# Attention on one core: the row totals are inverted in four pieces of 128 columns, two of them earlier in the macro step

## The reference

```python
h = _L0_tok_ref(x, L0_tok_weight)
scores = jnp.einsum('bqhe,bkhe->bhqk', q, k) / math.sqrt(D_HEAD)
scores = jnp.where(causal[None, None], scores, -jnp.inf)
pattern = jax.nn.softmax(scores, axis=-1)
z = jnp.einsum('bhqk,bkhe->bqhe', pattern, v)
h = h + attn_out                      # attn_out = z @ W_O + b_O, on _layernorm(h)
h = h + _L0_ffn_ref(_layernorm(h), ...)
```

## Time and profile before

| | |
|---|---|
| median of 3 runs | 2627.59 us (2624.28 to 2630.31) |
| profiled execution | 2633.09 us, of which the span of the instructions is 2631.4 us |
| PE busy over the span | 2369.2 us (90%), granted clock 0.963 on average |
| DVE busy | 1876.9 us (71%) |
| ACT and POOL busy | 1245.0 and 1245.7 us (47% each) |
| the inversions (L973) | 96 of 128 x 256, 167.5 us in all |

### The profile page before, as it was taken

One profiled execution on the slowest core, in us unless ns is written; L12 is line 12 of the kernel. 1 busy time (PEld: TensorE's weight loads), 2 busy tenths in 40 slices (PEclk: granted clock), 3 DMA queues, 4 the chain that ended last, 5 costly groups with the idle time before them and its releaser, 6 DMA issues. The chain is left out here.

```text
span 2631.4 us, 42687 instructions
## 1 busy us (share of the span) xinstructions
PE 2369.2 (90%) x16192; PEld 1254.9 (48%) x16192; DVE 1876.9 (71%) x3802; ACT 1245.0 (47%) x1760; POOL 1245.7 (47%) x858
## 2 busy tenths in 40 slices
PE   3564899999999999999999999986999999999998
PEld 1233556665656565656565665543333333333332
DVE  7864665756565756656565656687988888988987
ACT  3322233333333333333333333345777777787776
POOL 5000265767675757675766666653413413323120
PEclk9786999999999999999999999996999999999999
DMA  1002000000001000000000001132011001000000
GB/s 50 12 15 62 1 8 7 3 10 1 9 1 33 1 10 1 10 1 9 1 10 1 10 1 20 19 52 56 9 19 27 9 19 21 15 19 17 11 7 7
DMA packets 42941, 39.35 MB, mean 15 GB/s; under 512 B 26865, under 2 KB 35186, under 8 KB 41842
## 3 DMA queue, kind: packets, MB, share of 16 engines
q1 hardware_dynamic: 40608, 31.18, 5.4%
q0 software_dynamic: 1536, 3.15, 0.4%
q10 hardware_dynamic: 594, 2.31, 0.2%
HBM read 26.13 MB, written 10.49 MB: 14 GB/s over the span
## 5 line engine op out<-in xcount | busy, mean ns | idle before, releaser
L690 POOL TENSOR_TENSOR acc<-acc,pT 128x1024 f32<-128x1024 f32 (+3 forms) x412 | 837.9, 2034 | 228.5 <-ACT pT L1131 191.6
L1131 ACT ACTIVATE pT<-banks 128x1024 f32<-128x1024 f32 x480 | 406.8, 896 | 803.9 <-PE banks L769 758.3
L1868 DVE TENSOR_TENSOR hw<-hid,banks 128x512 f32<-128x512 f32 x1024 | 662.8, 680 | 86.4 <-PE banks L1551 71.9
L930 DVE TENSOR_REDUCE part<-banks 128x2 f32<-128x1024 f32 (+3 forms) x432 | 438.3, 1044 | 300.5 <-PE banks L745 298.6
L1710 ACT ACTIVATE hid<-banks 128x1024 f32<-128x1024 f32 x512 | 496.6, 1022 | 186.4 <-PE banks L1541 169.6
L785 PE MATMUL banks<-pT,v 128*64 128x512 f32 (+3 forms) x1920 | 405.7, 543 | 0.9 <-POOL pT L674 0.9
L1551 PE MATMUL banks<-wT,select 64*128 64x512 f16 x1024 | 342.8, 394 | 41.1 <-DVE hw L1868 21.4
L1541 PE MATMUL banks<-zst,w1c 50*128 50x512 f32 x1024 | 307.7, 545 | 12.7 <-ACT hid L1710 12.7
L1551 PEld LDWEIGHTS banks<-wT,select 64*128 64x128 f16 x1024 | 93.9, 94 | 398.5 <-DVE hw L1868 338.8
L1559 PE MATMUL banks<-hw,w 128*32 128x512 f32 x2048 | 278.3, 616 | 0.8 <-DVE hw L1868 0.8
L785 PEld LDWEIGHTS banks<-pT,v 128*64 128x64 f32 x1920 | 116.6, 136 | 194.6 <-issue 172.5
(11 more groups left out here) (243 smaller groups left out, 3239.5 us busy)
## 6 DMA issues: line engine op xcount, KB each, us to landing
zst<-z_scratch SPq DMA_DIRECT2D x48, 128.0 KB, 4.1
z_scratch<-zp SPq DMA_DIRECT2D x8, 512.0 KB, 2.8
out_h<-o SPq DMA_DIRECT2D x8, 384.0 KB, 2.6
xT_scratch<-xs_hi SPq DMA_DIRECT2D x4, 512.0 KB, 2.7
xt_hi<-xT_scratch SPq DMA_DIRECT2D x2, 1024.0 KB, 5.8
w<-in_L_ffn_W ACTq DMA_DIRECT2D x1, 2048.0 KB, 8.7
xt_hi<-in_L_ffn_W SPq DMA_DIRECT2D x12, 128.0 KB, 4.7
v<-in_L_ffn_W SPq DMA_DIRECT2D x12, 128.0 KB, 4.3
```

Of the source, the lines that this page charges most:

```text
L690: pool.tensor_tensor(acc[:, G % 2, :, off:CH], acc[:, G % 2, :, off:CH], pT[:, slot, :, 0:w], ALU.add).then_inc(summed, 1)
L930: last = dve.tensor_reduce(to[:, :, c:c + 1], both[:, :, 0:whole], AX.X, ALU.max)
L1131: act.activation(pT[:, J % PSLOTS, :, 0:CH - off], both[:, :, 0:CH - off], ACT.Exp, scale=E ** -0.5)\
L1868: dve.tensor_tensor(hw[:, n % 2, q, :], hid[:, n % 2, q, :], ring_bank(("w", g, n, q)), ALU.mult).then_inc(mixed, 1)
```

## The change

Every total is inverted in four pieces of 128 columns instead of two of 256. Pieces 0 and 1 belong to step a+2, pieces 2 and 3 to step a+3. Pieces 1 and 3 stand where the halves stood, at the end of the step; pieces 0 and 2 stand behind the first of the step's other items. Where the list of the step is empty (last unit), or where the first item is none of VectorE's, the piece stands ahead of everything that VectorE does in that step. The totals of the very last chunk are inverted in four pieces in a row.

```diff
-            def invert(it, Q, half):
+            def invert(it, Q, quarter):
                 G = it * NQC + Q
-                cols = slice(half * CH // 2, (half + 1) * CH // 2)
+                cols = slice(quarter * CH // 4, (quarter + 1) * CH // 4)
                 dve.wait_ge(total_copied, G + 1)
                 link(dve.reciprocal(total[:, G % 2, cols], total[:, G % 2, cols]))
...
-                    for item in PLAN[it][t]:
+                    for item in PLAN[it][t][:1]:
+                        side(item)
+                    for half in range(2):
+                        if behind(it, t, half + 2):
+                            invert(*behind(it, t, half + 2), 2 * half)
+                    for item in PLAN[it][t][1:]:
                         side(item)
...
                     if behind(it, t, 2):
-                        invert(*behind(it, t, 2), 0)
+                        invert(*behind(it, t, 2), 1)
                     if behind(it, t, 3):
-                        invert(*behind(it, t, 3), 1)
+                        invert(*behind(it, t, 3), 3)
                         normalise(*behind(it, t, 3))
...
-            for half in range(2):
-                invert(LAST, NQC - 1, half)
+            for quarter in range(4):
+                invert(LAST, NQC - 1, quarter)
```

## The result

| | before | after |
|---|---|---|
| median of 15 runs | 2630.31 us | 2621.47 us |
| ratio, 95% interval | | 0.9971 (0.9963 to 0.9979) |
| profiled execution, span | 2631.4 us | 2623.0 us |
| a steady unit (units 1 to 10 without 4) | 125.0 to 125.1 us | 124.4 to 124.6 us |
| unit 4 | 125.6 us | 124.8 us |

By the ratio the kernel became 7.6 us faster, between 5.5 and 9.7; the forecast was 6.5.

A forecast was written before the change was run, and what follows sets the result against it. TensorE was taken to bound the attention, with waits for VectorE at two places. Gains of 2.6 (site A), 3.7 (Site B) and 0.2 us (last unit) sum to 6.5: median 2627.6 - 6.5 = 2621.1 us, range 2617.5 to 2629.

The forecast's parts named there:

- What bounds the kernel: TensorE bounds the attention, busy 122.70 of 125.08 us a unit; it repeatedly waits for VectorE at two places, 2.38 us recoverable.
- The price of a piece: A 128-column reciprocal takes 949 ns, about 40 ns between linked ones; two quarters cost 0.19 us more than a half.
- site A: Chunk 1, steps 7 to 9, units 0 to 10: delayed cast finds GpSimd idle, 0.24 us a unit, 2.6 us gained.
- Site B: Chunk 2, steps 13 to 15: piece 0 hides in the cast's stall, step 15's 0.32 us wait goes, 3.7 us gained.
- The tight place at the third reduction: Step 14: third reduction ends at 646.12, TensorE wants its banks at 646.32; a slip of 0.1 us costs nothing.
- Chunks 0 and 3: Early pieces fit VectorE's idle time, no new TensorE wait; without that cover, at most 4.2 us lost for each chunk.
- The last unit: Output's wait of 1.78 us shrinks 0.6, later gain and loss equal, final inversion loses 0.4: net 0.2 us gained.
- Rival 1: Cast at site A doesn't shorten, so only Site B pays: 1.8 us gained, 2625.8 us; chance 0.18.
- rival 2: Casts are long by themselves at both sites, step 15's wait grows: 6.1 us slower, 2633.7 us; chance 0.06.
- Rival 5: What TensorE is spared it waits for later (ScalarE's exponentials, unit's end): no change, 2627.6 us; chance 0.09.
- Rival 3: At site A the moved cast runs into GpSimd's next addition if delayed over 1.6 us: 37 us lost, 2665; chance 0.02.
- Rival 4: Pieces' fixed cost paid in full, delayed second items holding up TensorE: 48 totals cost 18.7 us, 2646.3 us; chance 0.03.

The follow-up runs named there:

- the late quarters: Kernel before, with all totals inverted in quarters, both quarters of a step at its end, none early: ratio 1.0029, 7.6 us more.
- the whole half early: Kernel before, halves kept, only chunk 1's second half moved from the end of step 8 to behind its first other item: ratio 1.0135, 35 us more.
- The last edit above: The version with chunk 1's halves ahead, plus chunk 3's first half ahead of everything in the last unit's step 1: median 2612.73 us, ratio 0.9939.
- chunk 1 alone: Kernel before, with only chunk 1 (units 0 to 10) inverted in quarters, two of them early: ratio 0.9993, 1.8 us less.
- the reduction's experiment: Kernel before, with only the cast L948 written as a maximum over one element: ratio 0.9982, 4.7 us less.
- the version with chunk 1's halves ahead: Kernel before, chunk 1's halves ahead of step 7's first item and at its end, chunk 2 in quarters, last total in one piece: 2613.89 us, ratio 0.9935.

## Why the prediction was right, point by point

**What bounds the kernel.** Right: TensorE, and two places where it waits for VectorE. Two experiments that change one site each moved one of the two lines of waits and left the other.

**The price of a piece.** 944 ns instead of 949, with 40 ns between two as read. The 0.19 us for a pair is borne out by the late quarters: the wait at site A went from 1.44 to 1.63 us.

**Site A.** 0.24 us a unit forecast, 0.25 measured, by the cast's 0.43 less the quarters' 0.19. That the cast waited for GpSimd was read from two ends that agreed; the whole half early showed it.

**Site B.** The mechanism held, the size was a little off: 0.31 us of idle time a unit forecast, 0.37 us off step 15 measured (7.87 to 7.50 us in unit 2; 0.6 us in unit 4, as forecast). Over the 11 units site B gave 4.3 us and not 3.7. Why the step gains 0.06 us more than the idle time that went isn't shown. The tight place at the third reduction cost nothing that can be seen in the length of a unit.

**Chunks 0 and 3.** Nothing lost: averaged over units 1 to 10, steps 1 to 5 are each as long as before within 0.03 us.

**The last unit.** Here a step failed. I forecast 0.6 us less of waiting at its step 3, and it got 0.2 us longer. VectorE in step 1 there in the changed kernel, and GpSimd beside it:

```profile
1674.74 1.80 DVE L1007 TENSOR_TENSOR centred<-h_all,ln 128x768 f32<-128x768 f32 x1
```
```profile
1674.69 1.04 POOL L687 COPY acc<-pT 128x1024 f32<-128x1024 f32 x1 [1.47 <-issue]
```

By the shorter piece ahead of it L1007 came 0.05 us behind GpSimd's copy and was held for 0.8 us, all that the piece had won. I had applied the rule of the shared time to the cast and not to this subtraction, though it was in the same trace. The last edit above shows the other side of it. Later in the unit I had taken gain and loss as equal, and nearly so it came: step 18 got 0.4 us shorter and the stretch from there to the last inversion 0.5 us longer. In step 18 GpSimd's mask L674 took 0.45 us before; now it began 0.13 us behind VectorE's L1037 and took 2.48:

```profile
1750.05 2.34 DVE L1037 SCALAR_TENSOR_TENSOR w1c<-w1c,is_low,v 128x2048 fp32r<-128x2048 f32 x1
```
```profile
1750.18 2.48 POOL L674 TENSOR_SCALAR_AFFINE_SELECT pT<-pT 128x256 f32<-128x256 f32 x1 [2.46 <-ACT pT L1136]
```

I read it as the same exclusion with the roles exchanged; no experiment tests it. The end cost 0.4 us as forecast (3.92 instead of 3.54 us). So the last unit with the last inversion lost 0.6 us where I forecast a net gain of 0.2.

**The sum.** By the trace the change is worth 2.7 us at site A, 4.3 at site B and -0.6 in the last unit, 6.4 in all against a forecast of 6.5. That the sum is so close is luck in part: 0.6 us too little at site B and 0.8 us too much in the last unit cancel. The forecast of the median, 2621.1 us against 2621.47 measured, is as lucky: the runs before, 15 of them, have their median at 2630.31 us and not at the 2627.6 from which I subtracted.

**The rivals.** Rival 1 falls by chunk 1 alone, where site A pays 0.25 us a unit, and rival 2 by the casts of 0.17 us in the changed kernel and in the reduction's experiment. Rival 5 falls by the steady unit, which is 0.6 us shorter. Rival 3 is real but lies where it was put: at a delay of 1.785 us it happened, at 0.98 it didn't. That its price was close, 35 us against 37, is luck. The 3.4 us a unit were too much, since a half that is moved ahead of the cast no longer stands behind it (3.4 - 1.785 = 1.6; measured 1.7), and the other half of the loss was TensorE's clock, which I hadn't counted. Rival 4 is what the late quarters do, at 7.6 us and not 18.7: even there steps 1 to 5 kept their length, so chunks 0 and 3 paid nothing.

## What to carry to other kernels

Where two engines exclude each other for whole instructions, place the short instruction by the other's pauses: 0.8 us more of delay turned a gain of 2.7 us (by the trace) into a loss of 35, half of it by TensorE's clock. Splitting an instruction costs its fixed part each time (7.6 us here when nothing else changed), so it is worth it only to put a piece into idle time that exists, and for chunk 1 whole halves in idle time ahead of step 8 beat quarters inside it (17 us gained, with chunk 2 still in quarters, against 7.6). List for every moved instruction which ones it pushes against the other engine, not only the one under study.

## What was unexpected of the hardware

A wait of 2.74 us in front of TensorE was followed by some 6 us at 1.2 GHz in five of eleven units, by about half of that in two, and by none in four, with the same wait and the same work ahead of it. A shorter one, 1.9 us at the start of the attention, does it too in some executions: in the profile of the kernel before, the first projections ran at a granted clock of 0.66, in the profile after at 1.00. Busy time and clock of this stretch, before and after:

```profile
305.00:308.00 3.00, 3.00 (x12) 1.88 (x11) 0.00 (x0) 0.07 (x1) 2.66 (x4) 0.66 0.00 0
```
```profile
305.00:308.00 3.00, 3.00 (x18) 1.71 (x14) 1.13 (x1) 1.12 (x1) 1.69 (x3) 1.00 0.00 0
```

Step 1 of unit 0 took 9.24 us in the one and 7.68 in the other; of the ten traces here it took 9.24 us in one more and 10.70 us in the version with chunk 1's halves ahead, and 7.7 us in the rest, always behind the same wait of 1.9 us. What decides between them is open: I found nothing in these traces that tells the units with the drop from those without.
